# The last stage of a mixture layer, moved into the head steps of the attention layer after it

## The reference

```
xn = layernorm(x)
q  = l2_normalize_per_head(rms_norm(xn @ Wq.T) * q_norm_w)     # 4 heads of 64
o  = (silu(q @ w0.T) * (q @ w2.T)) @ w1.T                      # per head
s  = softmax(xn @ centroids.T + biases)                        # 16 experts, the 2 best kept
x1 = x + o + xn + sum_k s_k * (xn @ Wr[e_k].T + br[e_k]) + (xn @ Ws.T + bs) / 2
```

```
xn  = layernorm(x1)
h   = rms_norm(xn) * (gamma + 1)
a   = softmax(q k.T / 8) v  for 16 heads of 64, q, k, v = h @ w_qkv
out = x1 + a @ w_out + alpha * (xn @ ternary(W).T) + bias
```

## Time and profile before

| | us |
|---|---|
| median of 3 executions | 3307.8 (3302.02 to 3312.09) |
| the profiled execution, own time | 3308.2 |
| its span in the profile | 3306.1 |
| `route`, to about | 522 |
| `experts`, to about | 777 |
| `settle`, to about | 1071 |
| `phase_b`, to the end | 3306 |

### The profile page before, as it was taken

One profiled execution on the slowest core, in us unless ns is written; L12 is line 12 of the kernel. 1 busy time (PEld: TensorE's weight loads), 2 busy tenths in 40 slices (PEclk: granted clock), 3 DMA queues, 4 the chain that ended last, 5 costly groups with the idle time before them and its releaser, 6 DMA issues.

```text
span 3306.1 us, 49812 instructions
## 1 busy us (share of the span) xinstructions
PE 2888.7 (87%) x14674; PEld 2396.2 (72%) x14674; DVE 2162.8 (65%) x3501; ACT 1889.8 (57%) x2746; POOL 2153.1 (65%) x1384
## 2 busy tenths in 40 slices
PE   4878885894333899999999999999999999999997
PEld 4778774773232678888888888888888888888886
DVE  5777773334666667677666777666766767677664
ACT  3444432221121577677776777776777767677774
POOL 3666664004886377777777777777777777777775
PEclk7887775997555899999999999999999999999998
DMA  3222112555775222222222322222222222222221
GB/s 101 88 92 77 67 60 90 176 182 177 229 220 176 72 62 54 69 69 49 73 47 69 73 48 73 54 64 70 46 73 59 62 73 47 70 55 62 73 54 44
DMA packets 266850, 281.11 MB, mean 85 GB/s; under 512 B 96754, under 2 KB 205554, under 8 KB 266739
## 3 DMA queue, kind: packets, MB, share of 16 engines
q1 hardware_dynamic: 254452, 246.17, 27.9%
q0 software_dynamic: 12288, 33.57, 3.2%
HBM read 129.67 MB, written 82.31 MB: 64 GB/s over the span
## 4 chain that ended last, share of the span: by engine, by line
PE 64%; DVE 1%; ACT 1%; POOL 1%; DMA 1%; issue 0%; SPq 0%; POOLq 0%; ACTq 0%; DVEq 0%
PE psV_b L1609 7%; PE psV_b L1614 7%; PE psS_b L1597 7%; PE psS_b L1596 7%; PE psV_b L1610 7%; PE psN_b L1582 7%; PE psY_b L1537 4%; PE psX_b L1537 4%; PE psY_b L1538 4%; PE psY_b L1539 4%; PE psX_b L1539 4%; PE psX_b L1538 4%; POOL pp_lo_b L1328 1%; PE psN_b L1666 0%; DVE vals_lo_b L1505 0%
## 5 line engine op out<-in xcount | busy, mean ns | idle before, releaser
L1328 POOL TENSOR_TENSOR pp_lo_b<-pf_b,pp_hi_b 128x1024 fp32r<-128x1024 f32 x512 | 1227.9, 2398 | 603.8 <-ACT pp_hi_b L1370 516.7
L1473 DVE TENSOR_REDUCE negmax_b<-psN_b 128x2 fp32r<-128x1024 f32 x512 | 627.0, 1225 | 387.4 <-PE psN_b L1582 379.9
L1365 ACT ACTIVATE pf_b<-psS_b 128x1024 f32<-128x1024 f32 x512 | 526.4, 1028 | 237.2 <-PE psS_b L1597 233.8
L1596 PE MATMUL psS_b<-qA_b,kA_b 128*128 128x512 f32 x1024 | 405.9, 396 | 6.3 <-DVE qB_b L1488 4.4
L1597 PE MATMUL psS_b<-qB_b,kB_b 68*128 68x512 f32 x1024 | 406.4, 397 | 0.0
L1609 PE MATMUL psV_b<-pp_hi_b,vals_hi_b 128*128 128x512 f32 x1024 | 402.8, 393 | 1.4
L1610 PE MATMUL psV_b<-pp_hi_b,vals_lo_b 128*128 128x512 f32 x1024 | 402.3, 393 | 0.0
L1582 PE MATMUL psN_b<-kA_b,qA_b 128*128 128x512 f32 x1024 | 323.3, 396 | 4.6 <-DVE negmax_b L1473 4.5
L1614 PE MATMUL psV_b<-pp_lo_b,vals_hi_b 128*128 128x512 f32 x1024 | 318.0, 392 | 4.8 <-POOL pp_lo_b L1328 4.8
L1389 ACT ACTIVATE kA_b<-psX_b 64x512 fp32r<-64x512 f32 x256 | 152.2, 595 | 288.5 <-PE psX_b L1539 283.5
L1370 ACT ACTIVATE pp_hi_b<-pf_b 128x1024 fp32r<-128x1024 f32 x256 | 271.8, 1062 | 8.4
(11 more groups left out here) (248 smaller groups left out, 6815.6 us busy)
## 6 DMA issues: line engine op xcount, KB each, us to landing
kA_b<-kA_b SPq DMA_DIRECT2D x128, 256.0 KB, 3.1
qB_b<-qA_b SPq DMA_DIRECT2D x128, 256.0 KB, 2.9
inverse_b<-inverse_dram SPq DMA_DIRECT2D x256, 128.0 KB, 3.1
xs_e<-rows_dram SPq DMA_DIRECT2D x144, 128.0 KB, 2.1
results_dram<-ys_e SPq DMA_DIRECT2D x72, 256.0 KB, 2.3
x_a<-x_dram SPq DMA_DIRECT2D x16, 512.0 KB, 4.2
part_dram<-acc_a SPq DMA_DIRECT2D x32, 256.0 KB
acc_s<-part_dram SPq DMA_DIRECT2D x32, 256.0 KB
```

The source lines that it names most:

```text
L1328: pool.tensor_tensor(pp[1][:, c], pf[:, c], pp[0][:, c].bitcast(F32), ALU.subtract).then_inc(pl_pool, 1)
L1365: a.activation(pf[:, c], psS[:], ACT.Exp).then_inc(exp_act, 1)
L1473: v.tensor_reduce(negmax[:, n.slot(2), 2 * c:2 * c + 2], psN[:], AX.X, ALU.max, negate=True).then_inc(mx_dve, 1)
L1596: pe.matmul(psS[:, t], kA[:, s, keys], qA[:, s], start=True, stop=False)
```

## The change

`settle` is gone. Its work is done by `phase_b`, a tile at a time, one batch ahead, in a chain over several head steps (the tiles of batch b+1 in the steps of batch b). A tile whose transpose falls on step s of its batch's predecessor (s = 1, 4, 7, 9 by the table `FIRST`) is gathered by POOL some steps earlier (`GATHERS`) and loaded by SP (`LOADS`); DVE sums it at the end of step s-3; POOL takes the square roots at the start of step s-2; DVE makes the factors in step s-1, between the cast of the weights and qB's row; ACT applies them at the start of step s, PE transposes in a unit "F", ACT and DVE split, and SP stores at step s+1. The same unit multiplies the tile before with the ternary weights, so that tile's base is finished one unit later. Four tiles of batch 0 go through steps -22 to -4, before the first keys.

The table of units is new: V units stand in steps 0, 2, 3, 5, 6, 13, 14, 15, F units in 1, 4, 7, 9, and O units, now two output tiles each (24 matmuls, all 512 columns of psY), in 8, 10, 11, 12. Base and output move two tiles per DMA.

All steps are written out, in place of the loop. The value tile has 64 values and one column of ones for each head (65 columns) in its high part, 64 in its low part. Tiles that only the first two stages use are freed (`Sorted`).

```diff
+        UNITS = {0: ("V", 0, 3), 1: ("F", 1, 0), 2: ("V", 0, 4), 3: ("V", 0, 5), 4: ("F", 1, 1), 5: ("V", 0, 6),
+                 6: ("V", 0, 7), 7: ("F", 1, 2), 8: ("O", -1, 2), 9: ("F", 1, 3), 10: ("O", -1, 3),
+                 11: ("O", 0, 0), 12: ("O", 0, 1), 13: ("V", 1, 0), 14: ("V", 1, 1), 15: ("V", 1, 2)}
+        OS = 2 * (TB // U)
+        FIRST = {1: 0, 4: 1, 7: 2, 9: 3}
+        SD = 11
+        def tile_at(g, d):
+            k = g.const + d
+            if k % H not in FIRST:
+                return None
+            n = TB * (k // H + 1) + FIRST[k % H]
+            return n if 0 <= n < NT else None
+        GATHERS = {10: (0, 0), 11: (0, 1), 12: (1, 0), 13: (1, 1), 0: (2, 0), 1: (2, 1), 3: (3, 0), 4: (3, 1)}
+        LOADS = {12: 0, 15: 1, 2: 2, 5: 3}
...
         def for_steps(eng, step):
-            for g in range(-3, H):
-                step(Step(None, H, g))
-            if B > 2:
-                with eng.Fori(1, B - 1) as it:
-                    for h in range(H):
-                        step(Step(it, H, h))
-            for g in range(H * (B - 1), NH + 11):
+            for g in range(-22, NH + 11):
                 step(Step(None, H, g))
...
 @block.gpsimd, step(g), ahead of ot_lo and the first pp_lo:
+                if g.const % H in GATHERS:
...
+                        need(pool, s_dve, SD, n - 2, 3)
+                        pool.indirect_dma_start(out=fy[:, n % 2, k], out_offset=None, in_=results[:, :], ...)
+                n = tile_at(g, 2)
+                if n is not None:
+                    need(pool, s_dve, SD, n, 5)
+                    need(pool, s_dve, SD, n - 2, SD)
+                    pool.tensor_tensor(root[:, n % 2, 2:3], mv[:, n % 2, 1:2], eps, ALU.add).then_inc(s_pool, 1)
+                    need(pool, s_pool, 3, n, 1)
+                    pool.tensor_tensor(root[:, n % 2, 0:1], root[:, n % 2, 2:3], power[:, 0:1], ALU.pow).then_inc(s_pool, 1)
+                    pool.tensor_tensor(root[:, n % 2, 1:2], mv[:, n % 2, 1:2], power[:, 1:2], ALU.pow).then_inc(s_pool, 1)
...
 @block.scalar, start of step(g), and its end:
+                n = tile_at(g, 0)
+                if n is not None:
+                    need(a, s_dve, SD, n, SD)
+                    need(a, f_pe, 1, n - 1, 1)
+                    a.activation(fr[:], fsum[:, n % 3], ACT.Identity, bias=fac[:, n % 2, 4:5],
+                                 scale=fac[:, n % 2, 3:4]).then_inc(fr_act, 1)
+                def rows_high():
+                    if n is not None:
+                        need(a, f_pe, 1, n, 1)
...
+                        a.activation(ft[0][:]..., psY[:, 0, 0:D], ACT.Copy).then_inc(f_act, 1)
...
 @block.vector, step(g), after the cast and ahead of qB's row:
+                m = tile_at(g, 1)
+                if m is not None:
+                    f = fac[:, m % 2]
+                    need(v, s_pool, 3, m, 3)
+                    need(v, fr_act, 1, m - 2, 1)
+                    v.tensor_tensor(f[:, 0:1], root[:, m % 2, 0:1], root[:, m % 2, 1:2], ALU.mult).then_inc(s_dve, 1)
+                    v.tensor_scalar(f[:, 1:2], f[:, 0:1], 1e-12 * float(D) ** -0.5, None, ALU.max).then_inc(s_dve, 1)
+                    v.reciprocal(f[:, 2:3], f[:, 1:2]).then_inc(s_dve, 1)
+                    v.tensor_scalar(f[:, 5:6], f[:, 1:2], kept.alpha_bc[:, 0:1], None, ALU.mult).then_inc(s_dve, 1)
+                    v.tensor_tensor(f[:, 3:4], f[:, 2:3], root[:, m % 2, 0:1], ALU.mult).then_inc(s_dve, 1)
+                    v.scalar_tensor_tensor(out=f[:, 4:5], in0=mv[:, m % 2, 0:1], scalar=-1.0, in1=f[:, 3:4],
+                                           op0=ALU.mult, op1=ALU.mult).then_inc(s_dve, 1)
...
 the unit "F" on DVE (in odd steps ahead of qB's row):
+                            ins = v.scalar_tensor_tensor(out=base, in0=psY[:, 0, D:2 * D], scalar=fac[:, kk % 2, 5:6],
+                                                         in1=base, op0=ALU.mult, op1=ALU.add)
+                            v.tensor_tensor(ft[1][:]..., psY[:, 0, 0:D], ft[0][:]..., ALU.subtract).then_inc(f_dve, 1)
+                            v.tensor_tensor(base, base, fbias_bc[:], ALU.add).then_inc(fb_dve, 1)
...
 the end of DVE's step(g):
+                m = tile_at(g, 3)
+                if m is not None:
+                    total = fsum[:, m % 3]
+                    v.wait_ge(sums_in[m % 3], 16 * (m // 3 + 1))
+                    v.wait_ge(fx_in, 16 * (m + 1))
+                    v.tensor_tensor(total, total, fx[:], ALU.add).then_inc(s_dve, 1)
+                    v.wait_ge(gathered[m % 2], 16 * TOP * (m // 2 + 1))
+                    for k in range(TOP):
+                        v.scalar_tensor_tensor(out=total, in0=fy[:, m % 2, k], scalar=kept.share[k][:, m:m + 1],
+                                               in1=total, op0=ALU.mult, op1=ALU.add).then_inc(s_dve, 1)
+                    v.bn_stats(stats, total).then_inc(s_dve, 1)
+                    v.bn_aggr(mv[:, m % 2], stats).then_inc(s_dve, 1)
...
 @block.tensor, the unit "F":
+                        n = TB * b.const + number
+                        if n > 0:
+                            need(pe, f_dve, 1, n - 1, 1)
+                            for k in range(KD):
+                                pe.matmul(psY[:, 0, D:2 * D], ft[0][:, k], kept.wtern[:, k], start=(k == 0), stop=False)
+                                mm = pe.matmul(psY[:, 0, D:2 * D], ft[1][:, k], kept.wtern[:, k], start=False, stop=(k == KD - 1))
+                        if n < NT:
+                            need(pe, fr_act, 1, n, 1)
+                            for k in range(KD):
+                                mm = pe.transpose(psY[:, 0, k * P:(k + 1) * P], fr[:, k * P:(k + 1) * P], ident[:].bitcast(F32))
+                        mm.then_inc(f_pe, 1)
...
-        vals = [sb(f"vals_{p}", [P, TB, HP, 3 * DH], F32R) for p in ("hi", "lo")]
+        vals = [sb("vals_hi", [P, TB, H, DH + 1], F32R), sb("vals_lo", [P, TB, H, DH], F32R)]
...
-                    pe.matmul(psV[:, g.slot(2)], values(0, h, i), pp[0][:, c, t], start=(i == 0), stop=False)
-                    pe.matmul(psV[:, g.slot(2)], values(1, h, i), pp[0][:, c, t], start=False, stop=False)
+                    pe.matmul(psV[0:DH + 1, g.slot(2)], values(0, h, i), pp[0][:, c, t], start=(i == 0), stop=False)
+                    pe.matmul(psV[0:DH, g.slot(2)], values(1, h, i), pp[0][:, c, t], start=False, stop=False)
```

More of the change, by code:

```diff
@@ L106, in need, with route @@
         eng.wait_ge(sem, per * n + k)
-def route(nc, io, rows, part, region, jobs, kept, raw, raw_in):
+def route(nc, io, rows, part, region, jobs, kept, order, raw, raw_in):
     x_dram = io["x"].rearrange("(g t p) d -> g p t d", t=TB, p=P)
@@ L279, in const @@
                 own[0] += 1
-            for tile, value in ((kept.ident[:], 0.0), (masks[:, 0], 0.0), (masks[:, 1], 1.0), (masks[:, 2], 1.0), (masks[:, 3], 1.0)):
+            for tile, value in ((order.ident[:], 0.0), (masks[:, 0], 0.0), (masks[:, 1], 1.0), (masks[:, 2], 1.0), (masks[:, 3], 1.0)):
                 const(g.memset(tile, value))
@@ L717, in _ @@
                             three(out, [part[:, u % XT, t, k] for part in xt], [part[:, k] for part in wshare], k == 0, False)
-                        pe.matmul(out, kept.pick[:], bshare[:], start=False, stop=False)
+                        pe.matmul(out, order.pick[:], bshare[:], start=False, stop=False)
                         for h in range(FH):
@@ L735, in _, with experts @@
                     pe.matmul(psB[:, 0, 0:1], masks[:, 3], delta[:, 0:1], start=True, stop=True).then_inc(tern_pe, 1)
-def experts(nc, io, rows, results, region, jobs, kept, raw, raw_in):
+def experts(nc, io, rows, results, region, jobs, early, kept, order, raw, raw_in):
     with ExitStack() as ctx:
@@ L1262, in step @@
                 p = q_unit(g)
+                if g.const == -10:
+                    for c in range(len(STAGES), len(chunks)):
+                        sp.wait_ge(w_dve, KD * (c - len(STAGES) + 1))
+                        load_weights(c)
+                put(g)
                 if p is not None:
@@ L1613, in weigh @@
                     i = 2 * c + t
[L1614 removed]
+                    mm = pe.matmul(psV[0:DH + 1, g.slot(2)], values(0, h, i), pp[1][:, c, t], start=False, stop=(i == TB - 1))
                 mm.then_inc(pv_pe, 1)
@@ L1688, in two_layers @@
         early = Early(nc, ctx)
-        with ExitStack() as first:
-            kept = Kept(nc, first, N // P, jobs)
-            with ExitStack() as hold:
-                raw = hold.enter_context(nc.sbuf_tensor("wr_raw", [P, KD, NE * D], F32))
-                raw_in = hold.enter_context(nc.semaphore("wr_raw_in"))
-                route(nc, io, rows, part, region, jobs, kept, raw, raw_in)
-                experts(nc, io, rows, results, region, jobs, kept, raw, raw_in)
-            settle(nc, io, results, part, xT_hi, xT_lo, base, early, kept)
-        phase_b(nc, io, xT_hi, xT_lo, base, early)
```

(8 more changed lines are left out.)

458 lines of the change are left out of this document (187 added, 271 removed).

## The result

The changed kernel takes 3555.2 us (median of 4 runs, 3547.7 to 3562.7) where the kernel before takes 3308.7: ratio 1.075, 95% interval 1.072 to 1.078. The forecast was 3478 us: slower, as said, by 247 us where 170 were expected.

A forecast was written before the change was run, and what follows sets the result against it. PE's matmul stream bounds the second layer, its neighbours having 0.3 to 0.9 us slack. 3308.2 - 247 + 15 x 27.8 - 2.4 + 2.5 - 1 = 3478 us; own range 3400 to 3580, 8-in-10 range 3250 to 3595.

The forecast's parts named there:

- What goes: Before the second layer: 315.5 us from settle's first sum replaced by 69 us; gain 247 us, bounds 225 and 265.
- The port: Second-layer steps: DVE operations on two SBUF operands wait for POOL's running one; 12.2 us a batch on top.
- B: DVE's six small factor operations before qB's row in steps 0, 3, 6, 8: 1.25 us by themselves.
- only the order: Rival: in the batches only queue order costs, not the shared port; 15.7 us a batch, 3296 us; chance 0.22.
- the slack takes it: Rival: small blocks fall into DVE's and POOL's idle time, PE pays only its 42 us; 3102 us; chance 0.13.
- A and R, one chain: Steps 15, 2, 5, 7: DVE's sums and statistics (A) delay POOL's square roots (R) and work behind; 8.8 us a batch.
- F: DVE's block before qB's row, steps 1, 4, 7, 9: 0.48+0.42+0.36 us; held last sum adds 1.2 in 1 and 9.
- The clock: Rival: PE's clock falls after four gaps of 2 to 3.5 us a batch, 1.6 us each, 96 us: 3575; chance 0.12.
- PE's own work: Four matmuls and two transposes more per tile on PE in the batches: 0.7 us each, 42 us for 60 tiles.
- Values of 65 columns, unrolled steps, output in twos: Second layer: three parts of the change taken to cost nothing; the 65 columns with 30 us either way as bounds.
- the list: Forecast lengths of a batch's sixteen steps before the port's additions: 151.5 us for 135.9.

The follow-up runs named there:

- e1: The changed kernel with the three two-tensor operations of DVE's factor block written with one tensor and a per-partition scalar, same place: 3387 us.
- e12: The kernel of e9 with the three factor operations back to two SBUF tensors, same place and work: 216 us more than e9.
- e11: The kernel before, with unread DVE reductions (1024 and 400) ahead of qB's row in steps 0, 2, 4, 6, 8, 10 of 14 batches: 92 us more.
- e9: The work of e8, with adds, statistics, roots and some gathers moved to steps where POOL has a gap and data have landed: 3237.4 us.
- e8: The changed kernel with scalars in the factors, bias sum behind qB's row, gathered shares scaled on DVE and added to x on POOL: 3381 us.
- e10: The kernel before, with three unread DVE reductions of 1024 ahead of qB's row in steps 0 and 6 of 14 batches: 134 us more.

## Why the prediction was right, and what it left out

- **What goes** was right: 249.6 for 247.
- **The port** was right, and is shown by e1 and e12, which change the form of B's operands and nothing else. Operations of two SBUF tensors waiting for POOL's running one is what the rows of 1392, 1399 and 1457 show. Rival "only the order" (3296) falls; so does "the slack takes it" (3102): the price lay where the blocks stand, not in the sums of busy time.
- **A and R, one chain** was right in size (step 15: 10.84 for 10.9, 5: 11.15 for 11.8, 2: 9.73 for 9.6; in step 7 its two gaps are 0.70 + 1.53 = 2.2 for 2.3). It was incomplete: I let POOL's queue make `pp_lo` late, and did not ask what the cast does once `pp_lo` starts ahead of it. In steps 5 and 15 that stayed inside the forecast's numbers by chance.
- **F** is the first step that was mis-sized. I charged the held bias sum in steps 1, 9 and 5 and forgot 7, where it lasts 2.10 and PE waits 1.83 for the row behind it. That is step 7's 1.8.
- **The clock** is the term that was missing, and the reason why the forecast came out low. I kept it as a rival that replaces the forecast (3575, nearer to the result than my 3478), at 0.12, when it is a term beside the others: whatever tears the gaps brings it. The 33.4 us that a batch got longer are 21.4 of gaps, 6.6 of clock (half of 13.2), 2.8 of PE's own work (the forecast's 0.7 a tile, an estimate) and 2.6 left. With 14 gaps a batch that is about 0.2 for each, as in e11 (137.1 - 135.9 for six). In part it is the way a gap is counted: from the end of a record of 0.39 us, though the next matmul could have started 0.235 after it, so every gap reads 0.16 short and a wait under 0.16 is none. That it is all of it is not shown: e9 has 8 gaps a batch and 3.6 us left. The forecast's 27.8 had 3 of work and 25 of gaps: gaps 3.6 too high, the clock 6.6 and the unexplained rest 2.6 too low. 15 x 5.6 = 84 us, and 3478 + 84 = 3562, the profiled time (to the microsecond by luck, since what goes is off by 2.6 as well). Of the 49 drops 21 begin in steps 1 and 9, and there the medians show them: without a drop these steps took 9.89 and 9.81 to 9.90 (2 and 4 batches of 14), the forecast's 9.85, and with one 11.37 to 11.45. (Once, step 1 took 12.39.) The rival's own sum was near: 3.5 drops a batch (49 in 14) for its four, 1.9 us each (6.6 / 3.5) for its 1.6.
- **Values of 65 columns, unrolled steps, output in twos**: nothing, as said. Step 14 is 8.45 (8.48 before), and steps 10, 11 and 12 are 10.04, 9.90 and 9.81 for the list's 9.85, 9.8 and 9.85.

The cast needs a word, since it has one input and is held all the same. The Trainium skill (Advanced Engine Details and Errata, VectorE Performance Modes) says that casts and copies from SBUF to SBUF may run in a mode that takes both of DVE's ports, and that the second is shared with GpSimd. The trace agrees: the cast ends 0.55 to 0.6 after POOL's operation in every case above. e8's scaling of 256 elements, one input, is held as well: it took between 0.30 and 1.17, and where it spans the end of an operation of POOL it ends 0.15 behind that in the median.

At the lower clock matmuls start 0.43 apart and not 0.235, so about half of that time is lost. The Trainium skill (TensorE: Matmul & The Clock Gate, Terms) puts the penalty at the throttled time multiplied by the share of the clock that is gone, and the trace agrees. With half of the half-clock time taken off, the rest of the 11 kernels with the new second layer lies within 1.7 us of 141.3, and e10's 4.5 a batch stand against 145.6 - 135.9 - 5.6 = 4.1 measured.

**Open.** In batches 1 to 14 of all 14 kernels, a lower clock began between the start of a gap and 4 us after its end in 234 of 274 gaps of 2.3 us and more, in 159 of 441 of 1.5 to 2.3, and in 6 of 698 of 0.6 to 1.5. What decides in the middle no run here tells; nor do e10 and e11 tell whether the length of one gap counts or the idle time of a stretch, since both differ between them. Which of R and the cast costs what in step 5 was not separated.

## What to carry to other kernels

Before small work is put into the steps of a kernel that is bound by PE, ask of each instruction what runs on the neighbour at that instant: an elementwise operation on DVE that reads two tensors from SBUF, or casts inside SBUF, lasts until POOL's running one is over, however small it is; written with one tensor and a scalar, the same element took 0.2 us. That form is no cure at every size: at 256 elements it was held too. Price a gap of PE by its length and by the clock behind it: 1.1 us for one of about 1 us, 4.8 for one of about 2.7. And before a wait is moved away, look at what it keeps apart: R's wait at the head of POOL's queue was A's cover, and moving it cost 125 us, most of it by the clock behind the longer gaps.

## What the hardware showed that I had not expected

- A DVE operation of one element per partition is held for 1.9 us in the median of 64. Which of B's three pays depends on where POOL's next operation begins: 1392 took up to 1.28, 1399 up to 2.01, and 1401 0.16 in most cases and up to 2.32 in others.
- The hold is not one-sided: `otf` takes 1.68 at 2048.09, when the cast runs in its first half microsecond, and 1.27 where no such work of DVE stands beside it.
- Equal idle time, unequal price: 5.6 us a batch in two gaps cost 9.6 (134 / 14), in six gaps 6.6 (92 / 14).
